# Attention of a transformer tower: the turns of the maxima and of the heads move behind value products in TensorE's order

## What is computed

```python
q, k, v = jnp.split(qkv, 3, axis=-1)
logits = jnp.einsum('bhqd,bhkd->bhqk', q, k) / math.sqrt(HEAD_DIM)
attn = jax.nn.softmax(logits, axis=-1)
vals = jnp.einsum('bhqk,bhkd->bhqd', attn, v)
vals = vals.transpose(0, 2, 1, 3).reshape(B, S, EMBED_DIM)
return jnp.einsum('bse,oe->bso', vals, w_out) + b_out
```

## Time and profile before

| | us |
|---|---|
| median of 3 runs | 1179.73 |
| lowest and highest run | 1176.17, 1180.86 |
| the profiled execution's own time | 1175.91 |
| its span, first to last instruction | 1174.3 |
| TensorE matmuls busy | 1117.2 (95%) |
| VectorE busy | 913.8 (78%) |
| ScalarE busy | 590.7 (50%) |
| GpSimd busy | 400.8 (34%) |
| mean granted clock of TensorE | 0.985 |

### The profile page before, as it was taken

How to read it: one execution, slowest core, us unless ns; L and a number is a source line. 1 busy time by engine, 2 the same in 40 slices (tenths; PEclk the granted TensorE clock), 3 DMA queues, 4 the chain that set the end, 5 groups by cost and what they waited for, 6 DMA issues and landing times.

```text
span 1174.3 us, 22138 instructions
## 1 busy us (share of the span) xinstructions
PE 1117.2 (95%) x6022; PEld 710.9 (61%) x6023; DVE 913.8 (78%) x1567; ACT 590.7 (50%) x973; POOL 400.8 (34%) x516
## 2 busy tenths in 40 slices
PE   6998999999999999988999999977999999999996
PEld 3654333333333333466777877766888888888885
DVE  3788888888888888589888888777777777777775
ACT  3444777777777777642332221532444444444442
POOL 3011630101111011203454343453555555555553
PEclk9998999999999999999999999988999999999998
DMA  9886232323323233022454431312333333333332
GB/s 295 266 255 210 72 104 70 105 73 93 99 70 106 69 97 86 19 88 75 109 108 108 90 62 49 72 44 71 56 53 54 54 54 54 54 54 54 54 54 32
DMA packets 108691, 105.38 MB, mean 90 GB/s; under 512 B 42464, under 2 KB 97904, under 8 KB 108624
## 3 DMA queue, kind: packets, MB, share of 16 engines
q1 hardware_dynamic: 90528, 81.18, 24.5%
q0 software_dynamic: 18112, 23.57, 11.7%
HBM read 64.88 MB, written 39.68 MB: 89 GB/s over the span
## 4 chain that ended last, share of the span: by engine, by line
PE 70%; DVE 10%; POOL 5%; issue 4%; DMA 1%; ACT 1%; POOLq 0%; DVEq 0%; SPq 0%; ACTq 0%
PE mix_pairs L73 19%; PE by_key L662 11%; PE pv L673 11%; PE by_query L653 9%; PE mix_made L1820 8%; POOL kept_table L1102 4%; PE mix_turn L1807 3%; PE mix_made L1254 2%; PE mix_made L1242 2%; PE mix_turn L1787 1%; PE by_query L694 1%; DVE mix_stats L1432 1%; DVE k_mix_u L1442 1%; DVE mix_h L1428 1%; DVE mix_back L1485 1%
## 5 line engine op out<-in xcount | busy, mean ns | idle before, releaser
L746 DVE TENSOR_REDUCE k_neg_max<-by_query 128x2 f32<-128x1024 f32 x240 | 282.7, 1219 | 54.8 <-PE by_query L653 54.1
L806 ACT ACTIVATE k_wu_e<-by_key 128x512 f32<-128x512 f32 x512 | 278.4, 601 | 84.3 <-PE by_key L662 80.8
L662 PE MATMUL by_key<-k_wg_e 99*128 99x512 bf16 x512 | 180.4, 385 | 3.1 <-DVE pv L782 3.0
L1764 POOL DMA_INDIRECT out_rows<-x_y,k_slot x72 | 113.9, 1582 | 158.6 <-PE mix_turn L1787 109.8
L653 PE MATMUL by_query<-k_wg_e 96*128 96x512 bf16 x480 | 145.2, 383 | 0.2
L1862 ACT ACTIVATE x_gate<-mix_pairs 128x512 f32<-128x512 f32 x72 | 43.0, 597 | 200.9 <-PE mix_pairs L73 200.9
L673 PE MATMUL pv<-k_wu_e,k_wd_e 128*17 128x512 f32 x1024 | 134.5, 598 | 0.3 <-ACT k_wu_e L806 0.3
L662 PEld LDWEIGHTS by_key<-k_wg_e 99*128 99x128 bf16 x512 | 42.4, 97 | 144.2 <-ACT k_wu_e L806 80.8
L73 PE MATMUL mix_pairs<-w_short,x_T 128*128 x288 | 121.8, 423 | 2.0 <-issue 2.0
L1820 PEld LDWEIGHTS mix_made<-x_wd,x_acts_T 128*128 128x128 f32 x864 | 111.2, 188 | 7.4 <-ACT x_acts_T L1885 0.9
L73 PE MATMUL mix_pairs<-w_short,x_rest 128*128 x288 | 114.6, 398 | 0.0
(11 more groups left out here) (244 smaller groups left out, 1947.6 us busy)
## 6 DMA issues: line engine op xcount, KB each, us to landing
k_wg_e<-kept_qk SPq DMA_DIRECT2D x384, 64.0 KB, 2.1
kept_qk<-k_qk_parts SPq DMA_DIRECT2D x32, 384.0 KB, 3.2
kept_v<-k_v_ones SPq DMA_DIRECT2D x8, 544.0 KB, 6.0
k_wd_e<-kept_v SPq DMA_DIRECT2D x32, 136.0 KB, 2.6
k_wu_e<-in_xT POOLq DMA_DIRECT2D x8, 512.0 KB, 6.8
kept_heads<-k_wd_e SPq DMA_DIRECT2D x8, 512.0 KB, 3.0
k_heads_in<-kept_heads SPq DMA_DIRECT2D x8, 512.0 KB, 11.8
k_wg_e<-in_wg_e SPq DMA_DIRECT2D x8, 512.0 KB, 7.8
```

The lines of the kernel that those rows point to most:

```text
L662: pe.matmul(by_key[:, key_bank(job), :], k_rows[0:SROWS, g, h, kt * P:(kt + 1) * P], q_rows[0:SROWS, g, h, :], start=True, stop=True).then ...
L746: dve.tensor_reduce(neg_max[:, g % 2, 2 * n:2 * n + 2], by_query[:, bank:bank + 2, :], AX.X, ALU.max, negate=True).then_inc(query_read, 1)
L806: act.activation(probs[:, key_tile(j) // 2 * G + j // 2 % G, j % 2, :], by_key[:, key_bank(job), :], ACT.Exp, scale=float(HD) ** -0.5).the ...
L1764: pool.indirect_dma_start(out=dram["out"], in_=y[:, r % 2, :], in_offset=None, compute_op=ALU.add, out_offset=bass.IndirectOffsetOnAxis(ap ...
```

## The change

In the body of `unit` the two turns are written behind the value products of the same key tile instead of ahead of them, and TURN_HEADS becomes 11 instead of 12. With that, behind key tile 3 the products kt = 2 come first and the turn of the maxima second. The turn of the heads comes directly behind the products kt = 0, ahead of key tile 12. Instructions, waits and banks are the same.

```diff
@@ -641,7 +641,7 @@
     EARLY_PV = {11: 0, 15: 1}
 
     QUERIES = (0, 2, 2, 0)
-    TURN_HEADS = 12
+    TURN_HEADS = 11
 
     def tensor(pe, beside):
         def score_by_query(b, g, k):
@@ -712,14 +712,15 @@
                     if ahead:
                         score_by_query(b2, g2, k)
                     k += 1
+                if j in LATE_PV and prev:
+                    add_pv(bp, gp, LATE_PV[j])
+                if j in EARLY_PV:
+                    add_pv(b, g, EARLY_PV[j])
+
                 if j == MAX_BEHIND and next_max:
                     turn_max(b1, g1)
                 if j == TURN_HEADS and prev:
                     turn_heads(bp, gp)
-                if j in LATE_PV and prev:
-                    add_pv(bp, gp, LATE_PV[j])
-                if j in EARLY_PV:
-                    add_pv(b, g, EARLY_PV[j])
                 if not ahead:
                     beside(g, j)
```

## The result

The changed kernel takes 1169.41 us in the median of 6 runs (1168.52 to 1169.99), the kernel before 1179.3 (1175.76 to 1181.57) beside it. The ratio is 0.993, with a 95% interval of 0.9915 to 0.9946: between 0.5% and 0.9% faster. The profiled executions took 1169.99 after against 1175.91 before, 5.9 us less. The forecast was 1172.7 for the median and 1168.9 for an execution like the profiled one.

A forecast was written before the change was run, and what follows sets the result against it. TensorE's order bounds the attention, with stalls at the maxima's turn and the last queries. Steady units 4.7, later-division units 1.9, first and last batch 0.8, less 0.4, make 7.0 us: 1179.73 to 1172.7 us, range 1166.5 to 1178.5.

The forecast's parts named there:

- The releaser of the turn: Behind key tile 3, the turn of the maxima waits for GpSimd's last split of the maxima, not ScalarE: 0.24 us lost.
- the cover by the value products: At key tile 3, 0.985 us of the previous unit's value products hide GpSimd's 0.24 us of lateness.
- the slack: Time left between GpSimd's split and the moved turn of the maxima: 0.75 us, or 0.64 with the heads' turn moved too.
- Part A: At key tile 3, value products go ahead of the turn of the maxima: 0.195 us saved per unit, 0.165 in one of four.
- x: Step from the turn of the maxima to key tile 4: taken as 0.11 us, bounded by 0.055 and 0.155.
- rival R1: Both switches are cheap: x is 0.055 and the heads' longer weight load is hidden; 2.8 us more gained, 1169.9 us, chance 0.20.
- Part B: Heads' turn ahead of key tile 12: last queries stop waiting, saving 0.11 us per unit (0.20 in one of four), cost 0.046.
- The parts don't add: Removing the last queries' stall alone only lengthens TensorE's wait at the turn of the maxima; it pays only with that covered.
- The loss of 0.44 in the unit before the last: That unit has no queries, so key tile 12's 0.44 us delay through ScalarE is lost in full, once.
- Behind the attention nothing changes: After the attention, the mixing of the batches starts when it ends and shifts as a whole, with no change of its own.
- The base of the forecast: Starting times for the 7.0 us gain: runs' median 1179.73, giving 1172.7; profiled execution 1175.91, giving 1168.9.
- R2: The heads' division doesn't start earlier, so 3.7 us of the gain are missing: 1176.4 us, chance 0.15.

The follow-up runs named there:

- the shorter split: The kernel before, old order, with GpSimd's split of the maxima leaving out its last subtraction and ending 0.30 us earlier: 1168.67 us, ratio 0.9934.
- a still earlier split: The changed kernel with the last subtraction of GpSimd's split of the maxima left out, so that it ends 0.30 us earlier: 1171.79 us.
- part B alone: The kernel before with only the heads' turn moved ahead of key tile 12, the turn of the maxima left ahead of its value products: 1178.37 us, ratio 1.0012.
- both parts: The changed kernel, with both turns moved, against the kernel before: 1169.41 us, ratio 0.993; timed again, 1170.43 us, ratio 0.9925.
- Part A alone: The kernel before with only the turn of the maxima moved behind its value products, heads' turn behind key tile 12: 1168.6 us, again 1170.11 us.

## Why the prediction was right

The median of 1169.41 lies in the range of 1166.5 to 1178.5, and faster by over 0.5% was the likeliest of the three outcomes. Its mechanisms held; one term of its sum and the base it starts from were off, and that the number came as near as it did is in part luck, as the last three points say. Point by point:

- The releaser of the turn, the cover by the value products, the slack. Right: the shorter split shows the releaser, the turn starts 0.985 behind the products, and a still earlier split changes nothing.
- Part A's size, forecast at 0.195 us per unit. Measured 0.23 to 0.24. The term that was off is x, the step from the turn to key tile 4: 0.07 instead of 0.11, close to its lower bound of the earlier trace rows. That is one half of rival R1. So part A gives back nearly its whole stall, and not less as the prediction had it: key tile 3 to key tile 4 takes 1.36 us now, and 1.35 in the old order without the stall (the kernel with the shorter split).
- Part B's 0.11 and 0.20 less 0.046. Right with part A: in the changed kernel the step into pair 7 is 0.22, and the four turns of the heads take 0.49 instead of 0.44, the 0.05 being the longer first step behind the value products (0.165 instead of 0.11). So the other half of R1, that this cost is hidden, didn't come. The place of the cost was off: the heads' turn is recorded 0.985 behind the value products, not 1.03, and the cost shows one step later. That it is the weight load which makes this step longer is argued from its size. The Trainium skill (TensorE: Matmul & The Clock Gate, LDWEIGHTS) has the time of a weight load go by its columns alone and would put this cost at nothing; the trace doesn't agree, with 0.142 against 0.096 us for 128 columns.
- Together 0.31 and 0.38 us per unit (12.14 and 12.22 to 11.84) where 0.26 and 0.32 were worked out: 7.8 us in 24 units against 6.6. The attention as a whole, from 390.9 to 382.6 us, gave 8.3 where the sum said 7.0.
- The parts don't add. Right, and the sharpest statement of the prediction: part B alone gave 1.0012, and 0.094 us per unit on top of part A.
- The loss of 0.44 in the unit before the last. Right: 0.48 between the two kernels that differ in it.
- "Behind the attention nothing changes", and it shifts as a whole. Only nearly: the profiled span fell by 5.9 and not by 8.3, since the first stage ended 0.9 later in that execution and what follows the attention took 1.4 longer, with more stretches at half clock. For that reason 1168.9 lies only 1.1 below the profiled execution's 1169.99: the attention gave 1.3 us more than the sum, and what lies around it took 2.4 back. These two errors have nothing to do with each other, so this nearness is luck.
- The base of the forecast. Against the median the forecast stood 3.3 us too high, and R1's 1169.9 is the nearest number. Of the 3.3 us the attention accounts for 1.3. The rest is the base: a median of three runs of a kernel whose six runs on record reach from 1175.76 to 1181.57. Beside the second runs of both parts and of part A, five of its twelve runs took 1177.2 to 1178.0, with a mean clock of 0.983 to 0.987, six took 1180.8 to 1183.5, with 0.978 to 0.981, and one lay between. The changed kernel's first six runs had 0.983 to 0.988.
- What the time doesn't test. Part A alone has about the same median as both parts (1168.6 and 1170.11 against 1169.41 and 1170.43), and the range takes in R2, in which part B's gain fails. So the kernel's time would have been right without part B; what bears out part B are the steps and the periods.

## What to carry to other kernels

In a queue that sets the pace, add up start-to-start steps and ask for each step that is too long whose loop it closes: of two stalls on one loop, the earlier one can't be cashed in until the later wait is covered. A wait on a late engine is best covered by a long step that needs nothing from it, here one microsecond of value products; what it costs are the changed steps to the new neighbours, here at most 0.05 us. Keep such long steps spread out where other engines catch up behind them: joining two of them here took back more than the whole gain.

## What the runs showed of the hardware

- A turn of 128 bf16 columns leaves the next score only 0.07 us later at full clock, though a key tile's weight load is recorded with 0.096 us.
- The first of four fp32 turns (128 columns) directly behind value products takes 0.165 us to the second, against 0.11 behind a score. Their weight loads are recorded with 0.142 us, those of bf16 with 0.096, both of 128 columns.
- Two executions of part A alone differ by 1.9 us at the attention's start, one with the clock at half there (a key tile of 635 ns) and one without.
- Removing the switch between two groups of value products saved 0.21 us of TensorE's steps, and the waits that it caused cost 0.64.
